# One-hot matmuls find each slot's token, rows are gathered, and results go plainly into four planes (mixture-of-experts layer, 1 core)

## What is computed

```
n   = rmsnorm(x)                                  # 2048 tokens
p   = softmax(n @ gate_w.T); top 4, scaled to sum 1
y   = shared_down(silu(n @ sg.T) * (n @ su.T))    # shared expert, 352 wide
for each chosen (token, e):                       # 8192 pairs
    y[token] += p[e] * ((silu(n @ g[e].T) * (n @ u[e].T)) @ d[e].T)   # 176 wide
out = x_before + tanh(gate) * (x_after_attention + y)
```

## Time and profile before

| | us |
|---|---|
| median of 3 runs | 1999.33 (1997.53 to 2004.32) |
| the profiled execution | 1989.11 |
| its span, first to last instruction | 1987.3 |
| sorting stage, from its first SP issue to the first tile load | 1609.04 to 1756.11 |
| expert stage, to the end | 1756.11 to 1987.3 |

### The profile page before, as it was taken

One profiled execution on the slowest core, in us unless ns is written; L12 is line 12 of the kernel. 1 busy time (PEld: TensorE's weight loads), 2 busy tenths in 40 slices (PEclk: granted clock), 3 DMA queues, 4 the chain that ended last, 5 costly groups with the idle time before them and its releaser, 6 DMA issues. The chain is left out here.

```text
span 1987.3 us, 34326 instructions
## 1 busy us (share of the span) xinstructions
PE 1722.4 (87%) x11668; PEld 1455.4 (73%) x11668; DVE 1165.0 (59%) x2625; ACT 951.5 (48%) x2452; POOL 529.5 (27%) x527
## 2 busy tenths in 40 slices
PE   7998897697699999999992999999999969259993
PEld 6666664555688888888881788888888867258883
DVE  4688884698655656566546555555555457335553
ACT  2577776486355444545541444444454423225442
POOL 4133321243311111111111111111121114736663
PEclk7699997898899999999996999999999968679997
DMA  4111121265100100100002101001000043447666
GB/s 142 55 34 29 29 70 40 78 252 213 43 13 1 43 12 13 43 1 11 1 1 77 43 1 32 12 12 29 5 12 1 1 117 108 147 101 139 126 115 162
DMA packets 73274, 117.40 MB, mean 59 GB/s; under 512 B 8285, under 2 KB 59021, under 8 KB 71943
## 3 DMA queue, kind: packets, MB, share of 16 engines
q1 hardware_dynamic: 54014, 89.03, 14.4%
q0 software_dynamic: 14448, 19.80, 5.6%
q10 hardware_dynamic: 4648, 6.38, 1.0%
HBM read 86.65 MB, written 44.70 MB: 66 GB/s over the span
## 5 line engine op out<-in xcount | busy, mean ns | idle before, releaser
L1812 ACT ACTIVATE da_prob<-da_prob,da_nb,d_rqs 128x128 f32<-128x128 f32 x256 | 123.3, 483 | 260.2 <-DVE da_nb L2072 260.2
L1812 ACT ACTIVATE hold_wq<-hold_wq,ca_nb,c_rqs 128x128 f32<-128x128 f32 x256 | 123.4, 483 | 235.4 <-DVE ca_nb L2072 235.4
L653 DVE TENSOR_REDUCE a_mx<-a_s 128x2 f32<-128x512 f32 x256 | 167.1, 681 | 60.5 <-PE a_s L541 58.7
L470 ACT ACTIVATE a_prob<-a_s 128x512 f32<-128x512 f32 x256 | 147.4, 600 | 85.7 <-PE a_s L554 85.4
L1874 POOL TENSOR_TENSOR hold_wq<-hold_wq,ca_rsum 128x512 f32<-128x512 f32 x64 | 66.7, 1042 | 428.3 <-DVE ca_rsum L2077 428.3
L1874 POOL TENSOR_TENSOR da_prob<-da_prob,da_rsum 128x512 f32<-128x512 f32 x64 | 66.6, 1041 | 422.9 <-DVE da_rsum L2077 422.9
L2700 POOL DMA_INDIRECT slot_results<-t_ysb,t_dest x79 | 124.3, 1574 | 91.7 <-ACT t_ysb L2714 42.8
L554 PE MATMUL a_s<-a_qs,a_ks 32*128 32x256 f32 x512 | 101.6, 346 | 32.4 <-ACT a_prob L470 32.3
L1884 PE MATMUL da_qk<-d_xTh,da_wqkv_h 128*128 128x512 f32 x256 | 106.7, 417 | 6.4 <-DVE da_wqkv_l L2023 6.4
L541 PE MATMUL a_s<-a_ks,a_qs 32*128 32x256 f32 x512 | 101.0, 351 | 3.1 <-DVE a_mx L653 3.0
L2084 DVE SCALAR_TENSOR_TENSOR ca_oT_l<-ca_oT,ca_bv,ca_oT_h 128x512 fp32r<-128x512 f32 x64 | 48.0, 751 | 93.3 <-ACT ca_oT_h L1826 93.3
(11 more groups left out here) (412 smaller groups left out, 5610.2 us busy)
## 6 DMA issues: line engine op xcount, KB each, us to landing
t_xg<-slot_rows SPq DMA_DIRECT2D x79, 144.0 KB, 2.5
mw_raw<-in_d_expert_w SPq DMA_DIRECT2D x16, 352.0 KB, 6.1
slot_results<-in_d_fill SPq DMA_DIRECT2D x1, 4608.0 KB
a_heads<-a_osb SPq DMA_DIRECT2D x128, 32.0 KB
a_wraw<-a_heads SPq DMA_DIRECT2D x32, 128.0 KB, 2.1
mw_down<-in_d_expert_d SPq DMA_DIRECT2D x1, 2816.0 KB
hold_wk<-in_c_wkT SPq DMA_DIRECT2D x1, 2064.0 KB
hold_wq<-in_c_wqT SPq DMA_DIRECT2D x1, 2064.0 KB, 9.0
```

Of the source, the lines that this page charges most:

```text
L470: act.activation(prob[:, w % PR, :, :], s2[w % 2][:, :, :], ACT.Exp, scale=1.0 / A_ROOT)\
L653: dve.tensor_reduce(mx[:, b % 2, :, h], s1[s1_use(b, u) % S1_BANKS][:, :, :], AX.X, ALU.max)\
L1812: ins = act.activation(prob[:, p, b, :], prob[:, p, b, :], ACT.Exp, bias=nb[:, p, b:b + 1], scale=rqs[:, r:r + 1], accum_out=sums[:, p, b: ...
```

## The change

- Blank rows are no longer written; only row 0 of the DRAM buffer of rows is filled with zeros.
- `rows` (now 272 floats each: channels and weights) is stored once, plainly, to DRAM in token order (row 1 + token), and each tile gathers its 128 rows from there by a list of ids (`gather`, POOL). 16 tiles are gathered in the sorting stage, 8 at the start of the next, the others one per tile, 24 buffers in all.
- The list is made by matmuls. For each batch DVE makes two one-hot matrices per choice, lane (128 wide) and tile (80 wide); ACT multiplies the tile one by lane + 1, POOL by batch + 16 x choice; TensorE sums lane^T x tile over all tokens and choices into one 128 x 160 result, from which DVE computes ids and destinations (`identify`).
- A result goes to plane = the choice's number, row = token, so nothing is added in DRAM: plain indirect scatters. At the end four planes are loaded instead of two, in two sets of four buffers, and added on chip.

Cut to its core ("..." marks what is left out):

```diff
@@ bit_linear_ffn, SP
-                sp.dma_start(slots.rearrange("(u r) n -> u r n", r=Y_BUFS * P), ...)
-                sp.dma_start(results.rearrange("(u r) n -> u r n", r=Y_BUFS * P), ...)
+                sp.dma_start(slots[0:1, :], fill[0:1, :]).then_inc(filled, 16)
@@ constants
-ROW = DIM + META
+ROW = DIM + EXPERTS
+X_EARLY = BATCHES
+X_BUFS = BATCHES + 8
-PLANES = 2
+PLANES = 4
@@ ExpertWeights
+    def gather(self, pool, slots, t):
+        pool.indirect_dma_start(self.tile(t), None, slots[:, :],
+                                bass.IndirectOffsetOnAxis(self.ids[:, t:t + 1], 0)).then_inc(self.x_in[t % X_BUFS], 16)
@@ sort_and_share, SP (ahead of the loads of expert weights 5 to 15)
+                sp.wait_ge(meta_ready, 1)
+                sp.wait_ge(xn_ready, BATCHES)
+                sp.dma_start(slots[1:1 + BATCHES * TOKENS, :].rearrange("(b p) c -> p b c", p=P), rows[:, :, :])\
+                    .then_inc(rows_stored, 16)
@@ POOL
-                for b in range(BATCHES):
-                    for k in range(TOPK):
-                        n = TOPK * b + k
-                        after(pool, sent_rows[n % IN_FLIGHT], 16 * (n // IN_FLIGHT))
-                        pool.indirect_dma_start(slots[:, :], bass.IndirectOffsetOnAxis(idx[:, b, k:k + 1], 0),
-                                                rows[:, b, :], None).then_inc(sent_rows[n % IN_FLIGHT], 16)
-                for k in range(IN_FLIGHT):
-                    pool.wait_ge(sent_rows[k], ...)
+                for b in range(BATCHES):
+                    pool.wait_ge(tile_ready, b + 1)
+                    after(pool, found_psum, b - DEEP + 1)
+                    c = P + 1 + TOPK * b
+                    pool.tensor_tensor(named[:, b % DEEP, :, 1, :], in_tile[:, b % DEEP, :, :],
+                                       cons[:, c:c + TOPK].unsqueeze(2).broadcast_to([P, TOPK, TABLE]), ALU.mult)\
+                        .then_inc(block_ready, 1)
+                pool.wait_ge(rows_stored, 16)
+                pool.wait_ge(turned_psum, PAIRS)
+                pool.wait_ge(ids_ready, 1)
+                for n in range(X_EARLY):
+                    if n >= IN_FLIGHT:
+                        pool.wait_ge(first.x_in[n - IN_FLIGHT], 16)
+                    first.gather(pool, slots, n)
@@ TensorE
+                def find(b):
+                    pe.wait_ge(lane_ready, b + 1)
+                    pe.wait_ge(named_ready, b + 1)
+                    pe.wait_ge(block_ready, b + 1)
+                    for k in range(TOPK):
+                        mm = pe.matmul(f_ps, in_lane[:, b % DEEP, k, :], named[:, b % DEEP, k, :, :]..., ...)
+                    mm.then_inc(found_psum, 1)
...
+                    if 2 <= t < 2 + PAIRS:
+                        find(2 * (t - 2))
+                        find(2 * (t - 2) + 1)
@@ ACT
+                def name(b):
...
+                    act.activation(named[:, b % DEEP, :, 0, :], in_tile[:, b % DEEP, :, :], ACT.Copy, scale=cons[:, P:P + 1])\
+                        .then_inc(named_ready, 1)
...
+                    if 1 <= t < 1 + PAIRS:
+                        name(2 * (t - 1))
+                        name(2 * (t - 1) + 1)
@@ DVE
-                dve.tensor_scalar(idx[:, :, :], first4[:, :, 0:TOPK], -1.0, None, ALU.add).then_inc(idx_ready, 1)
+                chained(dve.tensor_scalar(tile_of[:, :, :], ...))          # three of these, then
+                chained(dve.scalar_tensor_tensor(lane_of[:, :, :], ...))
+                def locate(b):
+                    after(dve, found_psum, b - DEEP + 1)
+                    dve.tensor_tensor(in_lane[:, b % DEEP, :, :], ..., ALU.is_equal).then_inc(lane_ready, 1)
+                    after(dve, named_ready, b - DEEP + 1)
+                    after(dve, block_ready, b - DEEP + 1)
+                    dve.tensor_tensor(in_tile[:, b % DEEP, :, :], ..., ALU.is_equal).then_inc(tile_ready, 1)
...
+                    if t < PAIRS:
+                        locate(2 * t)
+                        locate(2 * t + 1)
...
+                    if t == PAIRS + 2:
+                        identify()
@@ routed_experts, SP
-                    sp.dma_start(xg[:, t % X_BUFS, :], slots[P * t:P * t + P, :]).then_inc(x_in[t % X_BUFS], 16)
...
+                for n in range(GROUPS):
+                    after(sp, added, PLANES * (n - 1))
+                    load_plane(sp, n, 0)
+                    load_plane(sp, n, 1)
+                    if n >= 1:
+                        store(n - 1)
@@ POOL
+                for t in range(X_EARLY, X_BUFS):
+                    if t >= X_EARLY + IN_FLIGHT:
+                        pool.wait_ge(x_in[t - IN_FLIGHT], 16)
+                    first.gather(pool, slots, t)
                 for t in range(NT):
                     pool.wait_ge(y_copied, t + 1)
-                    pool.wait_ge(dest_ready, t + 1)
-                    if t >= PLANES:
-                        pool.wait_ge(sent[(t - PLANES) % Y_BUFS], 16 * ((t - PLANES) // Y_BUFS + 1))
-                    d = t % D_BUFS
-                    pool.indirect_dma_start(results[:, :], ..., ysb[:, t % Y_BUFS, :], None, compute_op=ALU.add)\
+                    pool.indirect_dma_start(results[:, :], bass.IndirectOffsetOnAxis(first.dest[:, t:t + 1], 0),
+                                            ysb[:, t % Y_BUFS, :], None).then_inc(sent[t % Y_BUFS], 16)
+                    if t + X_BUFS < NT:
+                        pool.wait_ge(xT_psum, t + 1)
+                        pool.wait_ge(picked, t + 1)
+                        first.gather(pool, slots, t + X_BUFS)
@@ ACT, end
-                    load_plane(act, n, 1)
+                    after(act, added, PLANES * (n - 1))
+                    load_plane(act, n, 2)
+                    load_plane(act, n, 3)
@@ DVE
-                    dve.tensor_tensor(both[:, :, :], ...)      # mask_meta, pick_meta and place go
+                    dve.tensor_tensor_reduce(weighed[:, t % 2, :], xg(t)[:, DIM:ROW], first.pick[:, t, :], 1.0, 0.0,
+                                             ALU.mult, ALU.add, wd[:, t % D_BUFS:t % D_BUFS + 1]).then_inc(picked, 1)
```

More of the change, by code:

```diff
@@ L2198, in __init__ @@
         self.pick = s.sb("pick", [P, TABLE, EXPERTS], BF16)
+        self.rows = s.sb("rows", [P, X_EARLY, ROW])
+        self.ids = s.sb("ids", [P, TABLE], mybir.dt.int32)
+        self.dest = s.sb("dest", [P, TABLE], mybir.dt.int32)
+        self.x_in = [s.sem(f"x_in{k}") for k in range(X_BUFS)]
         self.ld_d = s.sem("ld_d")
@@ L2250, in sort_and_share @@
         rstd = s.sb("rstd", [P, BATCHES])
-        rows = s.sb("rows", [P, BATCHES, ROW])
+        rows = first.rows
         gw = s.sb("gw", [P, KT, 2, EXPERTS], F32R)
-        logits = s.sb("logits", [P, BATCHES, EXPERTS])
+        logits = wb[:, :].rearrange("p (b e) -> p b e", b=BATCHES)
         mx = s.sb("mx", [P, BATCHES])
@@ L2619, in routed_experts @@
 def routed_experts(nc, x_sb, ident, first, big, before, slots, results, out):
-    X_BUFS, D_BUFS = 6, 8
+    D_BUFS = 8
     with ExitStack() as stack:
         s = Scope(nc, stack, "t")
-        xg = s.sb("xg", [P, X_BUFS, ROW])
+        xg = first.tile
         xh = s.sb("xh", [P, 2, KT, P], F32R)
@@ L2630, in routed_experts @@
         ysb = s.sb("ysb", [P, Y_BUFS, DIM])
[L2631 to L2635 removed]
+        weighed = s.sb("weighed", [P, 2, EXPERTS])
+        wd = s.sb("wd", [P, D_BUFS])
+        own_pl = s.sb("pl", [P, 5, GB, DIM])
+        old_pl = first.raw[:, :, :].rearrange("p b c -> p (b c)")[:, 0:3 * GB * DIM]\
+            .rearrange("p (n b c) -> p n b c", n=3, b=GB)
+        pl = [own_pl[:, k, :, :] for k in range(5)] + [old_pl[:, k, :, :] for k in range(3)]
+        x0 = pl[0]
         xT_ps = [s.ps(f"xT{k}", [P, 2 * KT, P]) for k in range(2)]
@@ L2639, in routed_experts @@
         y_ps = [s.ps(f"y{k}", [P, 512]) for k in range(2)]
-        x_in = [s.sem(f"x_in{k}") for k in range(X_BUFS)]
+        x_in = first.x_in
         sent = [s.sem(f"sent{k}") for k in range(Y_BUFS)]
@@ L3012, in lay_out @@
     below = (lane[:, None] < lane[None, :]).astype(np.float32)
-    token = lane[:, None] + P * np.arange(BATCHES, dtype=np.float32)[None, :]
+    tiles = np.arange(TABLE)
+    spill = PLANES * PLANE + P * (tiles % Y_BUFS)[None, :] + lane[:, None]
     steps = np.concatenate([np.tril(np.ones((EXPERTS, EXPERTS), np.float32)).ravel(),
-                            np.arange(TABLE, dtype=np.float32)])
-    out["d_consts"] = np.concatenate([below, token, np.tile(steps, (P, 1))], 1)
+                            np.arange(TABLE, dtype=np.float32), lane + 1])
+    out["d_consts"] = np.concatenate([below, lane[:, None] + 1, np.tile(np.add.outer(np.arange(BATCHES), BATCHES * np.arange(TOPK)).ravel(), (P, 1)), np.tile(steps, (P, 1)),
+                                      -1 - spill, spill], 1).astype(np.float32)
     out["d_fill"] = np.zeros((Y_BUFS * P, ROW), np.float32)
```

(1 more changed line is left out.)

157 lines of the change are left out of this document (81 added, 76 removed).

## The result

The changed kernel takes **2029.89 us** (median of 4 runs, 2025.05 to 2035.22), the kernel before 1998.43 us (4 runs, 1989.50 to 2004.32): ratio 1.0165, 95% interval 1.0125 to 1.0206. It is 1.65% slower; I had forecast 1988 us. The profiled execution took 2026.51 us with a span of 2024.7 us, 37.4 us more than that of before.

A forecast was written before the change was run, and what follows sets the result against it. GpSimd's instructions bound the sorting stage, TensorE paced the expert stage, DMA bound the end. Terms -18.1 - 6.7 - 1.2 + 14.6 = -11.4 us gave 1977.7 profiled, median 1988 us, range 1970 to 2016.

The forecast's parts named there:

- A, blank rows: Ahead of the sorting stage: dropping two issues that write 16.5 MB changes 0, between -3 and 0 us.
- B, the token table: Shared expert's units: the table makes the tenth unit's product start 13.8 us later; ids ready at 1710.7 us.
- Rival 3: Sorting stage: the table holds VectorE for GpSimd's whole operations, 12.8 us instead of 6.4; 1994 us, chance 0.14.
- C, gathers instead of scatters: Sorting stage: 16 gathers at 1.44 us replace 64 scatters, 23 us; TensorE starts the expert stage 18.1 us earlier.
- the barrier: Between sorting and expert stages: 6.4 us from the last scatter's landing to the first load, which stays.
- Rival 1: All 79 gathers: each costs more than a plain scatter, 1.10 to 1.55 us; up to 2034 us, chance 0.18.
- D, the expert stage: Expert stage: GpSimd becomes the bound at 2.52 us for 55 tiles, 197.8 us against 204.5, -6.7.
- Rival 2: Expert stage: GpSimd's issues overlap or gaps shrink, TensorE keeps 2.26 us, 17.7 us less; 1977 us, chance 0.12.
- rival 4: Expert stage: a lower granted clock costs some 5 us; chance 0.06.
- E, the end: Loading and adding planes: 8.4 MB instead of 4.2, bound by DMA, +14.6 us, between 12 and 17.
- The landing: After the expert stage's last scatter: the planes' loads start 2.4 us later instead of 3.6, -1.2 us.
- The base: Whole kernel: the sum made in the profiled 1989.11 us, its difference laid on the runs' median of 1999.33.

The follow-up runs named there:

- chip B: Changed kernel with its 55 tile loads on SyncE, plus a second scatter or spare gather behind each of 55 scatters: 1983.7 and 1995.2 us (before 1990.9).
- the last experiment: Changed kernel with its 55 gathers spread over three in four steps and all plane parts loaded at once: 2017.0 us, ratio 1.0077.
- The fourth kernel: The kernel before with result scatters that overwrite instead of accumulate: 1997.4 us.

## Why the prediction was wrong

**A, blank rows: open.** Not separable: the start of the sorting stage varies by 20 us over the profiles, with the blank rows and without.

**B, the token table: the sum near, its parts not.** Counted from the stage's start, the last unit's gates come 11.0 us later than before (97.8 instead of 86.8); I had 13.8. The eight units with the table take 5.07 us each on average (1668.25 to 1708.77 us), not 5.6, so they cost 5.5 us instead of 10.8; ahead of them 5.4 us are lost instead of 3.0:

```profile
1668.25 0.60 ACT L2475 ACTIVATE e_silu<-e_turned 116x512 f32<-116x512 f32 x1 [1.50 <-DVE w_all L2549]
...
1708.77 0.60 ACT L2475 ACTIVATE e_silu<-e_turned 118x512 f32<-118x512 f32 x1 [3.69 <-PE e_turned L2432]
...
L2664 DVE TENSOR_TENSOR e_in_tile<-e_tile_of,e_steps 128x320 bf16<-128x320 f32 x16 | 11.9, 743 | 0.0
L2660 DVE TENSOR_TENSOR e_raw_gu<-e_lane_of,e_steps 128x512 bf16<-128x512 f32 x16 | 10.9, 679 | 0.0
L2361 POOL TENSOR_TENSOR e_named<-e_in_tile,e_cons 128x320 bf16<-128x320 bf16 x16 | 18.5, 1159 | 56.6 <-DVE e_in_tile L2664 56.6
```

The two comparisons cost 2 x (0.743 + 0.679) = 2.84 us a unit, 0.6 more than the 2.24 that I counted without GpSimd; I had added 0.8 for the two multiplications that run beside them. GpSimd's multiplications take 1.16 us each on the mean (0.72 to 1.82) instead of the 0.8 that I had estimated. Rival 3, which lets VectorE wait for whole operations, is false.

**C, gathers instead of scatters: right, with luck.** From the first issue (100.0 us after the stage's start) to the end of the sixteenth (124.6) it takes 24.6 us, forecast 23; the ids were ready earlier by about as much, so the end of the issues is just where I had it. What was off is the barrier: TensorE begins 3.5 us after the last issue ends, not 6.4; why is open. So -21.1 instead of -18.1. Six of the first eight gathers take 1.22 to 1.55 us, two beside VectorE's last hidden steps and four beside its weight splits; the rest take 0.94 to 0.95. Among these is one at 1731.40 us that lies wholly beside weight splits (1729.69 to 1732.39). It takes 0.94 us; so a weight split beside a gather doesn't always lengthen it, and that it is VectorE's instruction which lengthens the six stays likely and unproven, as ScalarE's splits and the loads of the weights run beside them too.

**Rival 1 is false:** gathers cost 0.97 us in the expert stage and 0.99 over all 79, below its 1.10.

**D, the expert stage: this step failed.** "0.96 + 0.30 + 0.96 + 0.30 = 2.52 us" is right as GpSimd's pace, and chip B shows a stage of just that pace (2.47 and 2.52). The error is in the wait: "who waits is ScalarE's copy, four result buffers on, and by it TensorE". ScalarE's copy waits for no scatter; what TensorE itself loses beside two indirect transfers a tile I had put at nothing, with no row that showed it. It is 0.5 to 0.9 us for each second transfer on chips A, C, D and E; on chip A 46 us for 55 (243.2 against 197.1), and in the first profiled execution the stage is nearly as long (240.0 us). I had a stretch that spoke for my view, TensorE fully busy beside scatters before 1696 us; but these come 1.42 us apart, and I had none of TensorE beside GpSimd at its undisturbed pace, since in the profiled execution it had nothing to do there. That gap I didn't see. Rival 2 (1977 us) falls with it. The 0.06 of rival 4 stood for some 5 us from a lower granted clock in the expert stage, an estimate that no run shows; the mean clock in the windows is 0.96 against 0.96 to 1.00 before, so it is at most a small part. That the pace fell to TensorE's 2.26 us after the last gather holds but for the steps at each sixteenth tile: 2.28. Whether TensorE's array stands still or only its reports are late stays open.

**E, the end: right, low by 2.8.** The landing cost 2.55 us (1983.95 to the first load at 1986.50) instead of the 3.6 before; I had 2.4. From the first load to the end it takes 38.2 us against 20.9, +17.3 where I had 14.6: 12.2 for the bytes by my estimate (4.2 MB at 343 GB/s; from 1987 to 2010 us it is 338), 2.7 for buffers by the last experiment, the rest is open.

```profile
1986.50 1.46 SPq L2751 DMA_DIRECT2D t_pl<-slot_results  x3
```

**The base.** I took the difference to a profiled execution of the kernel before that was 10 us below the median of its runs. The fourth kernel's sorting stage is 11.7 us longer, through TensorE's standstill; the usual execution of the kernel before may have this loss and the profiled one not. But the start of the sorting stage alone varies by 20 us, which would do as well. Neither is shown: the kernel before was profiled once.

No version that does the whole work beat the kernel before; 1.0077 is the nearest. The new sorting stage is worth its 21 us, the four planes cost 17 (some 15 with all loads at once), and what sinks the change is the second transfer a tile.

## What to carry to other kernels

Adding up one engine's instructions gives that engine's pace, not what its neighbours keep of theirs: before moving transfers to GpSimd's queue, look for a stretch of the trace in which TensorE had work beside GpSimd issuing at the density that the change will bring, and if there is none, put a price for it into the range. A stretch at a lower density is no proof: scatters 1.42 us apart cost TensorE nothing, and 1.25 to 1.3 us apart they held it up. Prefer SyncE's plain transfers for whatever has regular addresses: on chip A the stage took 197.1 us with the 55 tile loads on SyncE and 243.2 with them on GpSimd. And run a control on each chip: a variant that was harmless on one chip stalled on two others.

## What the runs showed of the hardware that was not expected

- On four of five chips, indirect transfers that follow each other at 1.25 to 1.3 us keep TensorE from making or reporting progress: 10 us of its work in 50 us of one sorting stage, 8 us at once beside twelve gathers in a row, 2 to 3 us at a time in the expert stage. A memset of the same occupation costs nothing (196.8 us of stage on chip E against 197.1 without it on chip A). With one indirect transfer a tile the pitch is 2.34 to 2.44 us on chip A (a kernel with none was not run); 28 extra cost 14 us, 55 cost 36 to 49. It doesn't matter whether they read SBUF (scatters) or write it (gathers): 240.8 and 244.1 us of stage on chip D.
- Which part of the indirect transfers holds TensorE up, their issue, the moving of their bytes or their reports, stays open. The DMA engines were a third busy (0.32 and 0.34 in the changed kernel's expert stage).
- The effect was there on four chips and not on one (1995.2 us against 2025.2 and 2034.2 us for the same kernel). The changed kernel itself was not run on that one, and each kernel had one execution there, so chip and chance aren't fully apart; on chip D all of 4, 4 and 4 executions agreed.
- A scatter that overwrites takes 0.96 to 1.01 us on the mean to issue, a gather 0.94 to 0.97 where nothing lengthens it, an accumulating scatter 1.55, with 0.30 between two.
